# Interleaving the rows of the stacked queries and keys, and moving the last gathers of a fused attention and mixture-of-experts kernel

## The reference, cut to what matters

```python
x = x + layernorm(attention(layernorm(x)))
x = x + layernorm(ffn(layernorm(x)))
# attention: 16 heads of width 16
q = ct_q @ w_up_q + rope(ct_q @ wq_r);  k, v alike from ct_kv
probs = softmax(q @ k.T / 4);  out = (probs @ v) @ wo
# ffn: token by token
shared = silu(x @ sh_gate) * (x @ sh_up) @ sh_down
routed = score * expert_top1(x)          # 8 experts, 256 -> 512 -> 256, one for each token
return shared + routed
```

## Time and profile before

| | |
|---|---|
| median of 3 runs | 431.63 us (431.09 to 433.25) |
| the profiled execution's own time | 429.76 us |
| its span in the profile | 427.9 us |
| PE busy | 397.9 us, 93% |
| DVE busy | 273.4 us, 64% |
| ACT busy | 208.1 us, 49% |
| POOL busy | 129.6 us, 30% |

### The profile page before, as it was taken

The page is one execution under the profiler, slowest core; times in us unless marked ns, Lnnn a source line. Parts: engine busy times, 40 slices in busy tenths (PEclk is TensorE's granted clock), DMA queues, the critical chain, the costliest instruction groups (busy, mean ns, idle before and its releaser), DMA issues.

```text
span 427.9 us, 9422 instructions
## 1 busy us (share of the span) xinstructions
PE 397.9 (93%) x3383; PEld 299.3 (70%) x3383; DVE 273.4 (64%) x629; ACT 208.1 (49%) x383; POOL 129.6 (30%) x184
## 2 busy tenths in 40 slices
PE   7998789999999999797989999999999999999990
PEld 6675456676776767374668999999994444589990
DVE  5674478787879786877475594222225898727775
ACT  1644647676675858555561112444446766311110
POOL 1423412516253434303211101212212220026872
PEclk9999899999999999899999999999999999999997
DMA  8899326364553736460127660011111111123422
GB/s 263 204 116 122 62 70 194 87 175 136 153 156 89 216 96 209 100 199 1 52 98 230 223 215 25 26 51 51 50 51 44 44 45 35 51 59 104 141 95 86
DMA packets 50756, 47.29 MB, mean 111 GB/s; under 512 B 5334, under 2 KB 45526, under 8 KB 50710
## 3 DMA queue, kind: packets, MB, share of 16 engines
q1 hardware_dynamic: 44779, 38.31, 34.2%
q0 software_dynamic: 1632, 4.46, 3.6%
q10 hardware_dynamic: 4299, 3.92, 2.7%
HBM read 25.19 MB, written 8.65 MB: 79 GB/s over the span
## 4 chain that ended last, share of the span: by engine, by line
PE 79%; DVE 8%; DMA 4%; issue 3%; ACT 3%; POOL 2%; ACTq 0%; DVEq 0%; POOLq 0%
PE bank L1388 40%; PE bank L1707 7%; PE bank L1392 6%; PE bank L1576 6%; PE bank L1556 5%; PE bank L1517 5%; PE bank L1732 3%; DMA stacks<-mT 2%; PE bank L1455 2%; DVE nmax L1057 2%; PE bank L1445 2%; PE bank L1503 1%; DVE wall L1087 1%; DVE stats_at L991 1%; POOL rstd_at L641 1%
## 5 line engine op out<-in xcount | busy, mean ns | idle before, releaser
L1057 DVE TENSOR_REDUCE nmax<-bank 128x2 f32<-128x512 f32 x112 | 74.4, 686 | 26.4 <-PE bank L1517 25.6
L1388 PEld LDWEIGHTS bank<-stacks,wall 128*128 128x128 f32 x512 | 59.8, 192 | 2.5 <-issue 1.9
L1388 PE MATMUL bank<-stacks,wall 128*128 128x128 f32 x512 | 61.2, 276 | 0.4 <-ACT stacks L909 0.4
L1263 DVE TENSOR_TENSOR stacks<-stacks,bank 128x512 f32<-128x512 f32 x34 | 23.3, 687 | 51.7 <-PE bank L1388 49.1
L873 ACT ACTIVATE pv<-bank 128x512 f32<-128x512 f32 x64 | 38.3, 603 | 36.7 <-PE bank L1576 35.8
L1576 PE MATMUL bank<-stacks 99*128 99x256 bf16 x256 | 49.5, 276 | 3.8 <-DMA stacks<-mT 3.3
L873 ACT ACTIVATE wall<-bank 128x512 f32<-128x512 f32 x64 | 38.5, 606 | 27.2 <-PE bank L1576 26.2
L909 ACT ACTIVATE stacks<-bank 128x512 f32<-128x512 f32 x34 | 20.3, 597 | 64.3 <-PE bank L1388 54.3
L1517 PE MATMUL bank<-stacks 96*128 96x256 bf16 x224 | 43.2, 278 | 6.4 <-DVE nmax L1057 6.2
L1388 PE MATMUL bank<-wall,stacks 128*128 128x256 f32 (+1 forms) x208 | 49.2, 380 | 0.0
L706 POOL DMA_INDIRECT stacks<-x_sc,row_i x18 | 19.9, 1105 | 89.5 <-PE bank L1392 70.5
(11 more groups left out here) (207 smaller groups left out, 795.4 us busy)
## 6 DMA issues: line engine op xcount, KB each, us to landing
stacks<-low_sb SPq DMA_DIRECT2D x144, 64.0 KB, 2.5
wall<-gate_up SPq DMA_DIRECT2D x8, 1024.0 KB, 5.4
wall<-down SPq DMA_DIRECT2D x8, 512.0 KB, 6.9
y_exp<-stacks ACTq DMA_DIRECT2D x18, 128.0 KB, 1.7
x_tok<-wall SPq DMA_DIRECT2D x8, 256.0 KB, 2.5
stacks<-x_tok SPq DMA_DIRECT2D x16, 128.0 KB, 2.5
out<-stacks SPq DMA_DIRECT2D x8, 256.0 KB, 2.1
stacks<-low_sb SPq DMA_DIRECT2D x12, 128.0 KB, 5.9
```

Of the source, the lines that this page charges most:

```text
L1057: dve.tensor_reduce(nmax[:, half, qt, 2 * pair:2 * pair + 2], two(sm_bank[u % 2]), AX.X, ALU.max, negate=True).then_inc(sm["sm_max"], 1)
L1263: dve.tensor_tensor(to, sg, fu[:, :], ALU.mult).then_inc(sm["h_sb"], 1)
L1388: last = pe.matmul(out_ap, lhsT, rhs, start=(n == 0), stop=(n == len(pairs) - 1))
```

## The change

The slots of `stacks` are laid out with a step: slot r took partitions 16r to 16r+15, and takes partitions r, r+6, r+12, ..., r+90. Both DMAs that fill it (L516, L536) are changed alike, for keys and queries, so the matmuls' contraction is over the same products in another order. The rows 96 to 98 stay.

At the end, `before_finals` issues three pairs' gathers instead of two, and each power is followed by the gather of pair c+3. Pair 6's sums are held in the first two tiles of `y_first`, which pairs 0 and 1 no longer need, so the wait for a store (`out_done0`) goes away there. `first_parts` is split: pair 6's first sum and statistics come before step LAST-1, ahead of VectorE's `hidden` in that step; pair 7's stay between the last two steps, behind `normalise(5)`.

```diff
         def z_of(c, p):
-            return z_last if isinstance(c, int) and c == HALF - 1 else z_sb[:, p, :, :]
+            if c >= HALF - 2:
+                return (y_first[:, 0:2, :], z_last)[c - HALF + 2]
+            return z_sb[:, p, :, :]
...
                 final(c, c // 2, c % 2)
+            between.get(LAST - 1, nothing)()
             single(LAST - 1)
             between.get(LAST, nothing)()
             single(LAST)
...
-                                    stacks[HD * r:HD * r + HD, b, side, :, :].rearrange("d h c -> d (h c)"),
+                                    stacks[r:ROWS:NSLOT, b, side, :, :].rearrange("d h c -> d (h c)"),
...
-                                        half_of(stacks[HD * r:HD * r + HD, b % 2, side, :, :], m),
+                                        half_of(stacks[r:ROWS:NSLOT, b % 2, side, :, :], m),
...
-                for c in range(2):
+                for c in range(3):
                     gather(c)
-            after_power = {c: c + 2 for c in range(HALF - 2)}
+            after_power = {c: c + 3 for c in range(HALF - 3)}
...
-            def first_parts():
-                for c in (HALF - 2, HALF - 1):
-                    dve.wait_ge(sm[f"gathered{c}"], 32)
-                    if c == HALF - 2:
-                        dve.wait_ge(sm[f"out_done{c % 2}"], 16 * (c // 2))
-                    dve.tensor_tensor(...); dve.bn_stats(...)
+            def first_part(c):
+                dve.wait_ge(sm[f"gathered{c}"], 32)
+                dve.tensor_tensor(...); dve.bn_stats(...)
...
             def between_last():
                 normalise(HALF - 3, 1)
-                first_parts()
-            run_ffn(dve, body, final, between={LAST: between_last})
+                first_part(HALF - 1)
+            run_ffn(dve, body, final, between={LAST - 1: lambda: first_part(HALF - 2), LAST: between_last})
```

More of the change, by code:

```diff
@@ L1311, in normalise @@
                                       ).then_inc(sm["zn_ready"], 1)
-            def first_parts():
-                for c in (HALF - 2, HALF - 1):
-                    dve.wait_ge(sm[f"gathered{c}"], 32)
-                    if c == HALF - 2:
-                        dve.wait_ge(sm[f"out_done{c % 2}"], 16 * (c // 2))
[L1319 to L1322, removed]
+            def first_part(c):
+                dve.wait_ge(sm[f"gathered{c}"], 32)
+                dve.tensor_tensor(z_of(c, c % 2)[:, 0, :], y_first[:, c, :], routed[:, c, :], ALU.add
+                                  ).then_inc(sm["z_ready"], 1)
+                dve.wait_ge(sm["z_ready"], HALF + c - 1)
+                dve.bn_stats(stats_f[:, c % 2, 0, :], z_of(c, c % 2)[:, 0, :]).then_inc(sm["out_stats"], 1)
             def last_part(c):
```

## The result

The changed kernel takes 427.41 us (median of 6 runs, 425.22 to 432.39), the kernel before, measured beside it, 432.50 (431.09 to 433.57). The ratio is 0.9872 with a 95% interval of 0.9843 to 0.9902: faster by 1.3%, some 5.5 us, where 3.2 us were forecast. The predicted 428.4 us is 1.0 us above the median; 0.9 us of that closeness is luck, since the forecast started from 431.63 us and the kernel before had 432.50 here. (The run of 432.39 is left out of the ratio: its mean granted clock was 0.971, where the others had 0.986 to 0.990.) Measured twice more, the changed kernel had 0.9862 (0.9817 to 0.9908) and 0.9888 (0.9852 to 0.9924).

The account below looks back on a forecast made before the run. TensorE was taken as the bound (79% of the chain), with gains only where it or the tail waits: 1.2 us at the start plus 2.0 at the end, 431.63 - 3.2 = 428.4 us, range 426.2 to 430.3.

Parts of the forecast that it names:

- Backlog at the start: Batch 0's start: interleaved rows leave no DMA backlog; head 0 0.95 us sooner, head 8 at about 45.0, 1.2 us gained.
- Rival B: Rows of `stacks`: the interleave gives nothing, the rate hangs on something else; 2.0 us gained in all, 429.6; chance 0.13.
- Later batches at 0: L536's 144 DMAs in later batches: off the path with 2.0 us to spare, so nothing counted.
- rival D: Later batches: spreading makes each DMA dearer; at 0.25 us more each, 2.8 us slower, 434.4; chance 0.05.
- Pair 7's gather and the 2.22 us of idle: End: pair 7's gather, issued one step sooner, lands at 414.2; VectorE's 2.22 us of idle before pair 7's first sum go.
- The collision at pair 7's first sum: End: POOL's addition for pair 5 holds VectorE's sum until 417.2; 2.0 us gained, against 3.2 without the stall.
- I take that stall: End: a sum at 405.46 that took 1.77 us instead of 0.42 beside POOL's addition, carried over to pair 7's first sum.
- rival A: End: VectorE and POOL don't collide at pair 7's first sum, or VectorE wins; 1.2 + 3.2 = 4.4 us, 427.2; chance 0.22.
- Third gathers ahead, cost 0: Last stage: two more gathers make POOL's first power 0.6 us later, hidden by VectorE's waits for TensorE; cost 0.
- Early sum ahead of `hidden`: Last step: pair 6's early sum makes `hidden` at most 0.25 us later, without delaying TensorE; 0.9 us gained behind `normalise(5)`.
- a sign of being wrong: Last step: the prediction called itself wrong if, among other signs, `hidden` of the last step delays TensorE's last product.
- rival C: Clock: the fall at 46.39 goes (4.9 us, 426.7) or one more comes (1.5 us, 430.1); chance 0.20, half each way.

Follow-up runs that it names:

- experiment 1: Kernel before with only the interleaved rows, in all batches (both edits of `stacks`), gathers and finishing order as before: 429.31 us, 0.9911.
- experiment 4: Kernel before with rows interleaved for batches 0 and 1 alone (edit of L516 only): 429.39 us, 0.9927 to the kernel before.
- experiment 5: Changed kernel with `stacks` slots at a step of two partitions instead of six: 425.89 us, 0.9868 to the kernel before.
- experiment 12: Changed kernel with every pair's sums written over its gathered rows (no wait for stores) and pair 6's first sum back behind `normalise(5)`: 426.1 us, 0.9864.
- experiment 3: Changed kernel without the early sum: pair 6's first sum and statistics back behind `normalise(5)`, between the last two steps: 427.42 us, 0.9886 to the kernel before.
- experiment 11: Changed kernel with every pair's sums written in place of its gathered rows, so no sum waits for a store; early sum kept: 425.23 us, 0.9812.
- experiment 9: The changed kernel again, code the same, to see what varies: 426.75 us, 0.9862 to the kernel before.
- experiment 7: Changed kernel with ACT's second pair of bias evacuations of batch 2 moved from head 5 to 6, second measurement: 427.99 us, 0.9909.

## Why the prediction was right, and where not

- **Backlog at the start: right.** The rate rose to the pace of issue, 200 GB/s (taken: anything above 202 leaves no backlog), the last stacks land 2.4 us after issue (27.0 us instead of 32.8), the maxima in 2.26 and 2.18 us where 2.73 was taken. Head 0 and head 8 stand within 0.25 us of the forecast 32.5 and 45.0, and head 8 waits for the step that was named, ACT's exponential: 1.0 us of the 1.2 that were summed for it. The 2.73 was the dearest of the usual ones (2.42 us on the mean), but TensorE's own work hid it. Rival B is out, by experiments 1, 4 and 5.
- **Later batches at 0: mis-sized by 0.4 us.** I had looked for a cost (rival D), with the cover of 2.0 us, and not for a gain: half a DMA in 2.0 instead of 2.5 us, and the maxima that go with it in 2.26 instead of 2.42. With half-clock stretches at the same places the rows are worth 1.6 us (experiment 12), not 1.2. That the forecast's profile has just 1.2 us at TensorE's end is luck: its stretches lie elsewhere and took some 0.3 us on balance. Rival D is out: L540 is issued as before (598 ns each, median) and lands sooner.
- **Pair 7's gather and the 2.22 us of idle: right.** The first sum of pair 7 has no wait on a DMA.
- **The collision at pair 7's first sum: wrong, 1.3 us.** The step that failed is "I take that stall". VectorE won with a start 0.17 us ahead, in all ten cases, so rival A's mechanism held: behind TensorE's end 3.3 us went, where that branch had 3.2 and the forecast 2.0. The row I went by was a sum with 0.18 us of lead that lost, and it was of the other kind: POOL's addition stood queued behind the gather issued at 404.7, where in the case that I forecast it stands alone. I had even written that down ("now is alone") and taken the row all the same. The two kinds are a pattern over 14 profiles. No run was made to test it, and why a queued addition holds a sum that starts before it stays open.
- **Third gathers ahead, cost 0: right on TensorE.** POOL's first power came 7.2 us behind the first gather instead of 6.6, the 0.6 us that were named, and TensorE's lead is 1.23 us all through the last stage: nothing on it moved.
- **Early sum ahead of `hidden`, "nothing there": right in part.** It held where nothing was late: `hidden` ends at 413.67, and TensorE's second half of the last step comes at 412.55 + 1.8 = 414.35. The slack I gave was one execution's. With the store late it is used up, and the early sum adds its 0.79 us to a pause of TensorE. `hidden` then delays the last product, which the prediction had named as a sign of being wrong; five of eight profiles show it. That chain (store, held sum, early sum, `hidden`) was the rival to name. From the start of TensorE's last product to the end of the span it is 13.0 to 13.8 us in those executions, where the old tail with a late store has 15.2 and 15.4 (experiments 4 and 1), and 10.8 to 11.2 in the others, where the old one has 14.1. So the change gains at either, 1.4 to 2.4 us or 3.0 to 3.3, but less where a store is late.
- **Clock: neither rival C nor its opposite.** The fall near 46.4 stayed and the other moved from 176 to 197 in two profiles of the changed kernel; the third has a single one, at 34. The same code has both, so it is spread and not shown to be part of the change. Two stretches that could be priced cost 1.1 and 1.5 us, within the 1.7 taken as the most.
- **Time.** The sum gives 3.2, the profiles 4.5, the medians' ratio 5.5. Between the first two stand the 1.3 us of the stall that did not come: 1.2 + 3.3 was measured for 1.2 + 2.0. The last 1.0 us lies within the interval (1.0 to 1.6% is 4.2 to 6.8 us).

Open: why experiments 1 and 4 show 3.8 and 3.2 us for rows that by the traces give 1.6 or less. Their intervals reach 2.4 and 1.6 us; falls of the clock and late stores, which differ between executions, are of that size, and no run separates them.

## What to carry to other kernels

When a small DMA is slow at one place only, look at what was issued before it: the windows' GB/s against the pace of issue tells a backlog, and a destination of 16 neighbouring partitions was the cause here. Before a piece of work is put ahead of an instruction that TensorE waits for, ask what is the latest that the engine can come to it, from more than one execution: the slack in one profile is not the slack. Split a difference at an instruction of the engine that sets the pace: the first gather waits for a landing, and split there the same 4.5 us would read as 1.6 and 2.9 instead of 1.2 and 3.3. And before a stall is carried over from a row, see what is queued in front of the other engine's instruction there and in the new place: a lead of 0.17 us won where the addition stood alone, and one of 0.18 us lost where it was queued.

## What the runs showed that I had not expected

- DMAs into 16 rows of `stacks`: 16 neighbouring partitions 121 GB/s, steps of two and of six alike 200 GB/s and not yet the limit (DMA share 0.73).
- VectorE's tensor_scalar on 128 x 2 elements, 0.17 us alone, took 1.04 us beside POOL's addition (411.26, over at 412.30, when the addition from 410.99 was over at 412.27); 1.18, 1.02 and 1.16 in experiments 3, 12 and 11. The Trainium skill (SBUF — State Buffer, section "Who interferes with whom") has tensor_scalar among the operations that can exclude GpSimd for a whole instruction, and holds that the one that starts first blocks the other. The rows agree on the exclusion. The order they don't bear out as the records show it: 20 sums started ahead of a queued addition and were held to its end.
- The sum of one PSUM and one SBUF input (L1328, L1359's first) took 0.41 to 0.43 us everywhere, beside POOL's addition too (415.03 beside 414.41 + 1.37).
- A store of 256 KB takes 2.1 us in the median and stood in the chains with 2.4 and 2.6 in one execution (experiment 9), and with 4.1 in another (experiment 7). A quarter of a us of that, by which pair 2's sum fell into POOL's addition or not, moved the end by 2 us.
